# Three 500-column matmuls after every product of the ODE stage, into PSUM columns that nobody reads

## The reference, cut to what matters

```python
def _mlp(y, W1, b1, W2, b2, W3, b3):
    h = jnp.tanh(y @ W1.T + b1)
    h = jnp.tanh(h @ W2.T + b2)
    return h @ W3.T + b3

def _rk4_step(y, dt, params):
    f = lambda z: _mlp(z, *params)
    k1 = f(y)
    k2 = f(y + dt / 2 * k1)
    k3 = f(y + dt / 2 * k2)
    k4 = f(y + dt * k3)
    return y + dt * (k1 + 2 * k2 + 2 * k3 + k4) / 6
```

## Time and profile before

| what | value |
|---|---|
| median of 3 runs | 9042.71 us (9041.32 to 9051.28) |
| the profiled execution's own time | 9044.94 us |
| its span, first to last instruction | 9043.1 us |
| mean granted TensorE clock over the span | 0.579 |
| PE, DVE, ACT, POOL busy | 5798.0, 5919.1, 2872.0, 1257.6 us |
| instructions | 361842 |

### The profile page before, as it was taken

One profiled execution on the slowest core, in us unless ns is written; L12 is line 12 of the kernel. 1 busy time (PEld: TensorE's weight loads), 2 busy tenths in 40 slices (PEclk: granted clock), 3 DMA queues, 4 the chain that ended last, 5 costly groups with the idle time before them and its releaser, 6 DMA issues. The chain is left out here.

```text
span 9043.1 us, 361842 instructions
## 1 busy us (share of the span) xinstructions
PE 5798.0 (64%) x136621; PEld 4855.8 (54%) x136621; DVE 5919.1 (65%) x33160; ACT 2872.0 (32%) x10559; POOL 1257.6 (14%) x5288
## 2 busy tenths in 40 slices
PE   7777466666666666666666666666666666655886
PEld 3333155555555555555555555555555555544675
DVE  5665466666666666666666666666666666545997
ACT  4444122222222222222222222222222222234886
POOL 1000011111111111111111111111111111101001
PEclk9888555555555555555555555555555555567897
DMA  3111000000000000000000000000000000002332
GB/s 117 62 64 46 10 3 3 3 3 4 3 3 3 4 3 3 3 4 3 3 3 4 3 3 3 3 4 3 3 3 4 3 3 3 4 0 88 118 120 88
DMA packets 39796, 183.74 MB, mean 20 GB/s; under 512 B 7107, under 2 KB 20998, under 8 KB 27926
## 3 DMA queue, kind: packets, MB, share of 16 engines
q1 hardware_dynamic: 25638, 92.62, 2.7%
q0 software_dynamic: 12400, 67.68, 2.0%
HBM read 122.66 MB, written 37.62 MB: 18 GB/s over the span
## 5 line engine op out<-in xcount | busy, mean ns | idle before, releaser
L593 PE MATMUL p<-H,W 128*128 128x8 f16 x130816 | 4172.6, 168 | 2540.8 <-DVE H L734 2528.0
L593 PEld LDWEIGHTS p<-H,W 128*128 128x128 f16 x130816 | 3821.3, 104 | 2892.1 <-DVE H L734 2879.0
L734 DVE SCALAR_TENSOR_TENSOR H<-h,H 128x8 f16<-128x8 f32 x10220 | 1502.6, 163 | 279.8
L669 ACT ACTIVATE h<-u 128x8 f32<-128x8 f32 x4088 | 851.8, 208 | 2495.2 <-DVE u L754 2300.5
L664 ACT ACTIVATE h<-r 128x8 f32<-128x8 f32 x4088 | 850.3, 208 | 2477.4 <-DVE r L762 2252.3
L754 DVE TENSOR_REDUCE u<-p 128x8 f32<-128x24 f32 x6132 | 1003.6, 175 | 838.4 <-PE p L593 838.4
L762 DVE TENSOR_REDUCE r<-p 128x8 f32<-128x24 f32 x4088 | 746.8, 183 | 1126.0 <-PE p L593 845.1
L729 DVE TENSOR_SCALAR H<-h 128x8 f16<-128x8 f32 x8176 | 1399.2, 171 | 38.8 <-ACT h L664 20.8
L569 POOL TENSOR_TENSOR twice<-r 128x16 f32<-128x16 f32 x511 | 109.5, 214 | 2931.5 <-DVE r L762 2931.5
L1170 PE MATMUL e_ph<-e_FX,e_W 128*128 128x256 f32 x1656 | 384.7, 396 | 89.4 <-DVE e_FX L1366 89.4
L1170 PEld LDWEIGHTS e_ph<-e_FX,e_W 128*128 128x128 f32 x1656 | 330.0, 200 | 142.5 <-issue 93.8
(11 more groups left out here) (326 smaller groups left out, 4624.9 us busy)
## 6 DMA issues: line engine op xcount, KB each, us to landing
e_W<-w_scaled SPq DMA_DIRECT2D x23, 2304.0 KB, 10.0
e_W<-w_scaled SPq DMA_DIRECT2D x23, 1152.0 KB, 5.2
raw<-in_spline POOLq DMA_DIRECT2D x24, 1024.0 KB, 7.0
w_scaled<-raw POOLq DMA_DIRECT2D x8, 2304.0 KB, 7.8
w_scaled<-raw POOLq DMA_DIRECT2D x8, 1152.0 KB, 10.0
raw<-in_base POOLq DMA_DIRECT2D x24, 128.0 KB, 7.0
raw_s<-in_scaler POOLq DMA_DIRECT2D x24, 128.0 KB, 7.5
rows_in<-zeros POOLq DMA_DIRECT2D x4, 768.0 KB, 16.5
```

The source lines that it names most:

```text
L593: ins = pe.matmul(out[:, m, 0:2 * B], W[:, q, k, P * m:P * m + P], H[:, k, :, :].rearrange("p q b -> p (q b)"), start=fresh[m], stop=(left ...
L669: sg.up(act.activation(cols(h2[:, e, :], q), cols(u2, q), ACT.Tanh, scale=scale), "h2")
L734: sg.up(dve.scalar_tensor_tensor(out=Hq[:, :, 1, :], in0=mb(cols(h, q)), scalar=HSCALE, in1=Hq[:, :, 0, :], op0=ALU.mult, op1=ALU.subtract ...
```

## The change

`keep_busy` issues three matmuls (FILL = 3), each with a weight load of its own, into bank k = 0, 1, 2 of a PSUM tensor, columns 12 to 511. Weights and moving data are both taken from `W2`, 500 fp16 columns of it. It is called twice per evaluation: after the product into `p2` it writes to `p1`, and after the product into `p1` it writes to `p2`, so always to the banks that the next product will use. Since DVE writes seeds to the same banks of `p1`, the three seed writes of a step now raise a semaphore "seeded", and PE waits for it before the fills into `p1`, except in evaluation 1, which has no seed write.

```diff
+    FILL = 3
...
-                    h2=4 * len(TANH2), hi2=4 * len(HIGH2), in2=4 * len(LOW2), l13_ps=4 * len(RED13), base=6, hsum=3, hist=1)
+                    h2=4 * len(TANH2), hi2=4 * len(HIGH2), in2=4 * len(LOW2), l13_ps=4 * len(RED13), base=6, hsum=3, hist=1, seeded=3)
...
+        def keep_busy(pe, out):
+
+
+            for k in range(FILL):
+                pe.matmul(out[:, k, 3 * B:S], W2[:, 0, k, 0:P], W2[:, 1, k, 3 * B:S], start=True, stop=True, skip_group_check=True)
...
                         product(pe, i, w, p2, W2, H1, "in1", LOW1, len(LOW1) * e, "l2_ps", RED2, BLOCKS2)
+                        if e != 1:
+                            wait(pe, "seeded", (1, 1, 2, 3)[e], w, i)
+                        keep_busy(pe, p1)
                         product(pe, i, w, p1, W13, H2, "in2", LOW2, len(LOW2) * e, "l13_ps", RED13, BLOCKS13)
+                        keep_busy(pe, p2)
...
-                            dve.scalar_tensor_tensor(out=seed(p1), in0=mb(r[:, 3, :]), scalar=1.0 / 3.0, in1=mb(hb[:]), op0=ALU.mult, op1=ALU.add)
+                            sg.up(dve.scalar_tensor_tensor(out=seed(p1), in0=mb(r[:, 3, :]), scalar=1.0 / 3.0, in1=mb(hb[:]), op0=ALU.mult, op1=ALU.add), "seeded")
...
```

More of the change, by code:

```diff
@@ L745, in _ @@
                         if e == 0:
-                            dve.scalar_tensor_tensor(out=seed(p1), in0=mb(r[:, 3, :]), scalar=1.0 / 3.0, in1=mb(hb[:]), op0=ALU.mult, op1=ALU.add)
+                            sg.up(dve.scalar_tensor_tensor(out=seed(p1), in0=mb(r[:, 3, :]), scalar=1.0 / 3.0, in1=mb(hb[:]), op0=ALU.mult, op1=ALU.add), "seeded")
                         elif e == 2:
-                            dve.scalar_tensor_tensor(out=seed(p1), in0=mb(r[:, 3, :]), scalar=1.0 / 6.0, in1=mb(hb[:]), op0=ALU.mult, op1=ALU.add)
+                            sg.up(dve.scalar_tensor_tensor(out=seed(p1), in0=mb(r[:, 3, :]), scalar=1.0 / 6.0, in1=mb(hb[:]), op0=ALU.mult, op1=ALU.add), "seeded")
                         elif e == 3:
                             wait(dve, "base", 6, w, i)
-                            dve.scalar_tensor_tensor(out=seed(p1), in0=mb(r[:, 2, :]), scalar=2.0, in1=mb(base[:]), op0=ALU.mult, op1=ALU.add)
+                            sg.up(dve.scalar_tensor_tensor(out=seed(p1), in0=mb(r[:, 2, :]), scalar=2.0, in1=mb(base[:]), op0=ALU.mult, op1=ALU.add), "seeded")
                         for n, q in enumerate(RED2):
```

## The result

The changed kernel takes 8909.57 us (median of 3 runs, 8903.25 to 8910.04) against 9042.71 before: ratio 0.9848, 95% interval 0.9826 to 0.987. Its profiled execution has a span of 8907.7 us where the one before had 9043.1, 135 less. The forecast was 8870, faster, with 173 less than the median of before; 133 came.

What follows compares the result with a forecast made beforehand. A chain of waits in the ODE stage, no engine full, was taken as the bound. 45 ns x 4088 products, 184 us, less 10 us for clock drops, gave 8870 us; own range 8720 to 9030, mostly 8780 to 8960.

Steps and rivals of the forecast that it cites:

- The fills fit: On PE between two products: at full clock three fills of 0.215 us occupy 0.67 of the 0.77 us standstill.
- The clock: TensorE's clock in the ODE stage: 1.00 from a few microseconds after the stage begins, and held there.
- Rival 4: End of the fill block on PE: fills outlast the standstill, 0.50 us per product, 11090 us; chance 0.18.
- The sum: Period of a product in the ODE stage: 45 ns less, times 4088 products, 184 us less.
- (a): Latency of a small matmul at L593 at full clock: between 0 and 41 ns less, 30 taken.
- (b): Spacing of a product's small matmuls: between 27 and 14 ns, upper end taken; 15 ns gained together with (c).
- (c): First start of a burst of small matmuls: 0 to 21 ns less; 15 ns gained together with (b).
- The second path: DVE's write of H's second half, needed by a product's 13th matmul: ready at 5004.64 against 5004.65, limiting a shorter start.
- The turns: Where the loop turns, seven times: the clock may drop, 20 products at 0.50 us more, 10 us.
- 1 (the product halves): Small matmuls: spacing 14 ns, latency 41 ns less, then other work binds; 8510 or 8450 us; chance 0.20.
- 2 (only the first of a burst gets shorter): First small matmul of a product: 20 ns x 4088 gained, 82 us less, about 8960 us; chance 0.10.
- 3 (nothing comes through): Clock up and fills hidden, but the second half of H holds the period at 1.62 us: 9045 us; chance 0.08.

Runs made afterwards that it cites:

- e3: The changed kernel with its three fills per product cut from 500 to 8 columns each: 9051.37 us, 1.0006 of the kernel before.
- e1: The changed kernel with two fills per product instead of three: 9304.73 us, 1.0283 of the kernel before.
- e10: The changed kernel with three fills into p1 and two into p2, of 500 columns: 10146.97 us, 1.1218 of the kernel before.
- e12: The changed kernel with three fills of 440 columns instead of 500: 10367.11 us, 1.146 of the kernel before.
- e6: The changed kernel with 24 probe matmuls (8, 32, 64 columns, and 8 with narrow weights) after every product into p1: 10320.55 us, one execution.
- e7: The kernel before the change, without fills, with the same 24 probe matmuls after every product into p1: 9526.8 us, one execution.

## Why the prediction was right, and where it was not

**The fills fit** at full clock: forecast 0.215 per fill and 0.10 us to spare, measured 0.21 and 0.14. The choice of half the f32 price per column was right. The price at half clock was forecast as 0.415 per fill and a period of 2.12; 0.39 and 2.11 were measured behind the turns. The added instructions and the wait for "seeded" cost nothing (e3).

**The clock** rose, 17 us into the stage and not a few, and held between the turns, as forecast, but the reason given was wrong. The prediction took PE's busy share as the sign, from a stretch with 3.40 of 3.40 us busy at 0.50 before a rise. In stretches of 100 us without a turn of the loop e1, e10 and e12 have PE busy for 99.8 us or more at 0.50, and they never rose. The earlier trace rows could not tell these apart: its fully busy stretch holds f32 matmuls of 128 columns alone, about 420 ns each, and the one of 6.34 in 8.10 ends on f32 matmuls of 512 columns. Here 40% of a period and more goes by in 8-column matmuls, whose records (168 ns long, 27 apart) overlap and count as busy throughout. The doubt that the prediction named in one sentence, whether this mix would do, was the right question. That three fills of 500 columns were enough was luck, as far as the reason given goes: three of 440 were not. Rival 4, with its chance of 0.18, had the right mechanism for what happens then, fills that outlast the standstill at 0.50. With fewer or shorter fills than the change has, e10 came to 10147 and e12 to 10367; the 11090 it named was for the full three.

**The sum** was 45 ns per product, measured 38; its terms failed in opposite ways, and that they made up for each other is luck. (a) Latency: 30 forecast between ends of 0 and 41, 2 measured. The step that failed is carrying part of the f32 difference over; the sentence beside it, that L593's 161 ns was already near the warm 165, had the answer. The sign that the prediction named for it, matmuls near 140 ns, did not come: they last 166. The Trainium skill, TensorE: Matmul & The Clock Gate, section "Single matmul latency", gives 169 ns warm for 8 columns. The 166 of this trace is 3 ns below, so by that rule the term was nothing, as it nearly is. (b) and (c): 15 forecast, 36 measured, 9 by the first gap of a product and 30 by a spacing of 25.0 instead of "a shade below 27", less 3 at the second path. The Trainium skill, same page, section "Wait — 56ns, not 53.3ns?", has a floor of about 25 ns from start to start. The traces agree, with 25.0 at the high clock for 8 and for 32 columns. With both rules, as the prediction works them out, the term would have been 38 and the forecast about 8900, an estimate by the page's figures. The byte rate by which I excluded 14 ns is not borne out: narrow weights, a quarter of the bytes, do not come closer (e6).

**The second path** was said to stop most of (c). It did less: the second half's last write starts at 5003.21, takes 0.17 and, with the prediction's 0.06 to reach PE, is there by 5003.44; the 13th matmul would start at 5003.13 + 0.01 + 12 x 0.025 = 5003.44. The two paths stayed level: the second costs products into `p2` 6 ns in the median and products into `p1` nothing.

**The turns** were forecast at 10 us, 20 products at the low clock. The trace has 35 of them, start included, for 15 us; with 5 us of longer standstills and 7 of products held up elsewhere it is 27. These 17 us more and the 7 ns per product that are missing, 29 us, less the 7 us that came from outside the stage, make 39 of the 40 us between 8870 and 8910. The time lies in the narrow range of 8780 to 8960.

**Rivals.** 1 (the product halves) is out: e6 shows no start closer than 25 ns in the median, at any width. 2 (only the first of a burst gets shorter) had the latency right and missed the spacing; of its 21 ns the first gap gave 9. 3 (nothing comes through) fell: the period is not 1.62.

## What to carry to other kernels

A standstill can be filled with idle matmuls to raise TensorE's clock, but first ask what the clock gives the work on the path: small matmuls were 25 ns apart instead of 27 and 2 ns quicker to finish, so doubling the clock brought 2.3% of a period. Where the filler does not lift the clock it is worse than nothing, because at the low clock it takes nearly twice as long and outlasts the standstill it was made for: 12% fewer columns turned 1.5% faster into 15% slower. Judge whether the clock will rise from stretches with the same mix of matmuls, not from PE's busy share, and keep long standstills (a turn of the loop) out of the stage.

## What the runs showed of the hardware that was not expected

- With PE busy for 99.9 of 100 us between the turns of the loop, the granted clock stayed at 0.50 for the whole stage, 7 to 8 ms, in three kernels (e1, e10, e12).
- Pairs of weight load and matmul started 25 ns apart at 2.4 GHz and 26.7 at 1.2 GHz, for 8 and for 32 columns, and for weights of 128 and, in the median, of 32 columns; the first pair with another weight width came 120 and 172 ns after the one before (e6, e7).
- From the start of an 8-column fp16 matmul in a stream to the DVE instruction that waits for it, 203 ns pass at 2.4 GHz and 205 at 1.2 GHz; by its record it lasts 166 and 168. Matmuls of 500 columns start 0.21 and 0.39 us apart.
